# Attention 1: the maxima of the scores from 32 rows per head instead of 96

## The chip, the cores and the metric

The kernel runs on one core of a Trainium2 chip. The metric is the device time of one execution in microseconds, taken as the median of several runs. The whole kernel is one launch that computes eight sublayers one after the other (attention 1, a spiking feed-forward, a state space block and others); the change touches only the first, attention 1, which fills about the first 440 us of some 2070.

## The reference, cut to what matters

```python
# x: (2, 1024, 128); 16 heads of 64; latent of 32
q      = einsum('bld,dhk->blhk', x, Wq)
latent = einsum('bld,dc->blc',  x, Wkv_down)
k      = einsum('blc,chk->blhk', latent, Wk_up)
v      = einsum('blc,chk->blhk', latent, Wv_up)
attn   = einsum('bqhd,bkhd->bhqk', q, k) / 8
attn   = softmax(where(causal, attn, -big), axis=-1)
out    = einsum('bqhd,hdo->bqo', einsum('bhqk,bkhd->bqhd', attn, v), Wout)
```

The softmax needs a number per query that is near the maximum of its scores, so that no exponential overflows. Any number near the maximum gives the same result, since it is divided out again.

## The kernel before, in words

**Heads and halves.** Queries are multiplied by `Wk_up` beforehand, so that a head's query has only 32 numbers (`LD`) and all heads share the latent as keys. Four heads make a group `gg` (0 to 7: two batches of four groups). A group's queries come as one 128 x 512 product per half of the sequence (items "q"), rows 32h to 32h+31 for head h. ScalarE rounds it to the matmul's type (`qh`, high half) and VectorE takes what is left (`ql`, low half). Twelve DMAs per group (`s0_spread`, L474 to L476) lay these out as `qst`: for each head rows 0 to 31 high, 32 to 63 low, 64 to 95 high again, rows 96 and 97 the negated maximum in two halves. `kst` holds the latent in the same way (high, high, low, ones). One matmul over 96 rows thus gives the score with all three cross products, and over 128 rows the score less its maximum.

**Two kinds of work are woven into 96 steps.** A step `t` = (gg, c, n) handles half c of the queries (512) against block n of 128 keys, for the four heads. The numbers of steps below are t modulo 12: a group has steps 0 to 3 for c = 0 and 4 to 11 for c = 1. A step is: scores transposed, one matmul per head or two or four heads in one where the block is narrow (`scores`, L532, with a mask product L535 on the diagonal), exponentials on ScalarE (L695) from three PSUM banks in turn (3, 4, 5), and the products with the latent (`values`, L548, four heads in four groups of 32 columns), while GpSimd adds up the exponentials (L755).

Meanwhile the *items* prepare the maxima of the group that follows. "f" is a full block of 128 queries by 512 keys for one head: one matmul (L581) and one `tensor_reduce` on VectorE (L813). "d" is a block on the diagonal, r = 0 to 3 with width 128(r+1): four heads in one bank for r = 0, two for r = 1, one for r = 2 and 3; each is its product (L573), then a mask product (L576), then the reduce (L825). "n" transposes the negated maxima (L587), which then go to `qst` by DMA. "z" are the softmax sums (L599, L604), "y" the output. Items use PSUM banks 0, 1 and 2 in turn: item i waits until item i-3 has been read (`s0_af` at least i-2).

**The order is fixed by a plan.** `PLAN[t]` lists the items of a step, `plan(..., quota)` deals them out. In the turn of twelve steps that prepares a group they are, from step 3 on: 4, 4, 3, 3, 3, 3, 4, 4, 5, 5, 1, 1 items, to which come a "z" in steps 1 and 5 and a "q" in steps 10 and 11. The list is the 11 diagonal items of c = 0, "n", 16 full ones, 11 diagonal ones, "n". `parts(t)` cuts a step's items in thirds, and TensorE does: scores of two heads, first third, values of step t-1, second third, scores of the other two heads, last third. Before the steps there is an opening, which does the queries, latents and the maxima of group 0.

VectorE, ScalarE and GpSimd take the items in the same order, each on its own queue, with semaphores between them.

Of the kernel before, what the change touches and what calls it, by code (L numbers as in the profile page):

```python
# [7 lines left out]
ALU = mybir.AluOpType  # L8
# [6 lines left out]
P = 128  # L15
# [35 lines left out]
def f32(ap):  # L51
    return ap.bitcast(F32)


def build(nc, a, out, upto=8):

    ctx = ExitStack()
    with ctx:
# [281 lines left out]
        wkv4 = [tr(P), tr(P)]  # L340
        kst = tr(B, L)
        qst = [tr(2, 4, 512), tr(2, 4, 512)]
        qh = tr(2, 512)
        ql = tr(2, 512)
        nh = tr(2, P)
        nl = tr(2, P)

# [10 lines left out]
        s0_lat = sem("s0_lat")  # L358
        s0_khi = sem("s0_khi")
        s0_klo = sem("s0_klo")  # L360
        s0_latc = sem("s0_latc")
        s0_a = sem("s0_a")
        s0_qhi = sem("s0_qhi")
# [43 lines left out]

        def diagonal(gg, c):

            return [("d", gg, c, r, h, n) for r, n in ((0, 4), (1, 2), (2, 1), (3, 1)) for h in range(0, 4, n)]  # L410

        def full(gg):
            return [("f", gg, r, h) for r in range(4) for h in range(4)]
# [16 lines left out]
        for gg in range(2, NG0):  # L430
            t0 = 12 * (gg - 1)
            plan([("q", gg, 0), ("q", gg, 1)], (t0 - 2, t0 - 1), (1, 1))
            plan(diagonal(gg, 0) + [("n", gg, 0)] + full(gg) + diagonal(gg, 1) + [("n", gg, 1)],
                 range(t0 + 3, t0 + 15), (4, 4, 3, 3, 3, 3, 4, 4, 5, 5, 1, 1))
        for u, t in LAST.items():
            PLAN[min(t + 2, N_STEP + 1)].insert(0, ("z", u))
# [6 lines left out]
        def parts(t):  # L443

            x = PLAN[t]
            if len(x) == 1 and x[0][0] == "n":
                return [], [], x
            k = (len(x) + 2) // 3
            return x[:k], x[k:2 * k], x[2 * k:]

        def count_of(kind, i):
            return sum(1 for x in ITEMS[:i + 1] if x[0] == kind)
# [10 lines left out]
        def s0_spread(q):  # L463

            q.wait_ge(s0_pad, 4)
            for i, x in enumerate(ITEMS):
                if x[0] == "q" and x[2] == 1:
                    gg = x[1]
                    q.wait_ge(s0_af, i + 1)
                    if gg >= 2:  # L470
                        q.wait_ge(s0_e, SLOT_OF[12 * (gg - 1)])
                    for h in range(4):
                        rows = slice(LD * h, LD * h + LD)
                        q.dma_start(f32(qst[gg % 2][0:32, :, h, :]), f32(qh[rows])).then_inc(s0_qd, 16)  # L474
                        q.dma_start(f32(qst[gg % 2][32:64, :, h, :]), f32(ql[rows])).then_inc(s0_qd, 16)
                        q.dma_start(f32(qst[gg % 2][64:96, :, h, :]), f32(qh[rows])).then_inc(s0_qd, 16)  # L476
                if x[0] == "n":
                    _, gg, c = x
                    u = 2 * gg + c
                    q.wait_ge(s0_af, i + 1)  # L480
                    for row, part in ((96, nh), (97, nl)):
                        q.dma_start(f32(qst[gg % 2][row:row + 1, c, :, :].rearrange("o h (r q) -> o (h r) q", q=P)),
                                    f32(part[0:16, u % 2, :]).unsqueeze(1)).then_inc(s0_nd, 16)

        def s0_pe(pe):
# [53 lines left out]
            def values(t):  # L539
# [15 lines left out]
                                        start=n == 0, stop=n == 4 * c + 3, skip_group_check=True)  # L555
                ins.then_inc(s0_pv, 1)

            def item(x):
                i = AT[x]
                wait(pe, s0_af, i - 2)  # L560
                o = bank(i % 3)
                if x[0] == "q":
                    _, gg, k = x
                    b, g = gg // G0, gg % G0
                    ins = mm3(pe, o, (wq4[0][:, P * g:P * g + P], wq4[1][:, P * g:P * g + P]),
                              xt(L * b + 512 * k, 512))
                elif x[0] == "d":
                    _, gg, c, r, h, n = x
                    w = P * (r + 1)
                    pe.wait_ge(s0_qd, 192 * (gg + 1))  # L570
                    v = o[:, 0:n * w].rearrange("p (h k) -> p h k", h=n)
                    for k in range(n):
                        pe.matmul(v[:, k, :], qst[gg % 2][0:96, c, h + k, P * r:P * r + P],  # L573
                                  kst[0:96, gg // G0, 512 * c:512 * c + w], start=k == 0, stop=True,
                                  skip_group_check=True)
                    ins = pe.matmul(v[:, :, w - P:w], ident_bf[:, :],  # L576
                                    causal_bf[:, :].unsqueeze(1).to_broadcast([P, n, P]), start=False, stop=True,
                                    skip_group_check=True)
                elif x[0] == "f":
                    _, gg, r, h = x  # L580
                    ins = pe.matmul(o, qst[gg % 2][0:96, 1, h, P * r:P * r + P], kst[0:96, gg // G0, 0:512],  # L581
                                    start=True, stop=True)
                elif x[0] == "n":
                    _, gg, c = x
                    u = 2 * gg + c
                    pe.wait_ge(s0_m, u + 1)
                    ins = pe.matmul(o[0:16, 0:P], negf[:, u % 4, :], ident[:, :], start=True, stop=True)  # L587
                elif x[0] == "z":
                    u = x[1]
                    if (u // 2, u % 2) == PE_SUMS:  # L590
                        pe.wait_ge(s0_pv, N_STEP)
                        pe.sem_inc(s0_a, 1)
                        return
                    pe.wait_ge(s0_zp, ADDS_TO[LAST[u] + 1])
                    last = [t for t in range(LAST[u] - 2, LAST[u] + 1) if late(t)]
                    if last:
                        pe.wait_ge(s0_e, SLOT_OF[LAST[u] + 1])
                    for h in range(4):
                        ins = pe.matmul(o[LD * h:LD * h + LD, :], ones32, zacc[u % 2][:, h, :], start=True,  # L599
                                        stop=not last, skip_group_check=True)  # L600
                    for t in last:
                        c0, w = width(t)
                        for h in range(4):
                            ins = pe.matmul(o[LD * h:LD * h + LD, c0:512], ones32, pt[t % 4][:, h, 0:w], start=False,  # L604
                                            stop=t == LAST[u], skip_group_check=True)
                else:
                    _, b, k = x
                    pe.wait_ge(s0_ot, 2 * G0 * (b + 1) - (1 if k < 2 else 0))
                    for t in range(2):
                        for g in range(G0):  # L610
                            q0 = 256 * k + P * t
                            ins = pe.matmul(o[:, P * t:P * t + P], ot[:, g, q0:q0 + P], bcomb[:, g, :],
                                            start=t == 0 and g == 0, stop=g == G0 - 1, skip_group_check=True)
                ins.then_inc(s0_a, 1)
# [4 lines left out]
            latents(0)  # L619
            latents(1)  # L620
            pe.wait_ge(s0_klo, 2 * B)
            pe.wait_ge(s0_latc, B)
            pe.wait_ge(s0_pad, 4)
            for x in PLAN[-1][2:]:
                item(x)
            for t in range(N_STEP + 2):
                first, second, third = parts(t)
                own = range(len(slots(t))) if t < N_STEP else []
                for j in own[:2]:
                    scores(t, j)  # L630
                for x in first:
                    item(x)
                if 0 < t <= N_STEP:
                    values(t - 1)
                for x in second:
                    item(x)
                for j in own[2:]:
                    scores(t, j)
                for x in third:
                    item(x)  # L640

        def s0_act(act, link):
            act.preload_act_table_set("natural_log_exp_and_others")
# [25 lines left out]
            def latents(b):  # L669
                for i in range(2):  # L670
                    act.wait_ge(s0_lat, 3 * b + i + 1)
                    act.activation(kst[0:96, b, 512 * i:512 * i + 512], bank(LAT_BANK[b][i])[0:96],
                                   ACT.Copy).then_inc(s0_khi, 1)
                act.wait_ge(s0_lat, 3 * b + 3)
# [24 lines left out]
            def item(x):  # L699
                i = AT[x]  # L700
                if x[0] == "q":
                    _, gg, k = x
                    act.wait_ge(s0_a, i + 1)
                    wait(act, s0_qd, 192 * gg)
                    act.activation(qh[:, k, :], bank(i % 3), ACT.Copy).then_inc(s0_qhi, 1)
                if x[0] == "n":
                    _, gg, c = x
                    u = 2 * gg + c
# [53 lines left out]
        def s0_dve(dve, link):  # L762
# [13 lines left out]
            def item(x):  # L776
                i = AT[x]
                o = bank(i % 3)
                if x[0] == "q":
                    _, gg, k = x  # L780
                    dve.wait_ge(s0_qhi, count_of("q", i))
                    wait(dve, s0_qd, 192 * gg)
                    dve.tensor_tensor(ql[:, k, :], o, f32(qh[:, k, :]), ALU.subtract).then_inc(s0_af, 1)
                elif x[0] == "n":
                    _, gg, c = x
                    u = 2 * gg + c
# [27 lines left out]
                else:  # L814
# [2 lines left out]
                    dve.wait_ge(s0_a, i + 1)  # L817
                    v = o[:, 0:n * w].rearrange("p (h k) -> p h k", h=n)
                    if c == 0:
                        if r == 0 and u >= 4:  # L820
                            dve.wait_ge(s0_a, AT[("n", gg - 2, 0)] + 1)
                        at = negf[:, u % 4, :].rearrange("p (h r) -> p r h", r=4)[:, r, h:h + n]
                    else:
                        at = negp[:, gg % 2].rearrange("p (h r) k -> p r k h", r=4)[:, r, 1, h:h + n]
                    dve.tensor_reduce(at, v, AX, ALU.max, negate=True).then_inc(s0_af, 1)  # L825
                    if r == 3 and h == 3:
                        dve.wait_ge(s0_af, i + 1)
                        if c == 0:
                            dve.sem_inc(s0_m, 1)
# [2033 lines left out]
```

## Time and profile before

| | us |
|---|---|
| median of three runs | 2062.61 (2062.19 to 2077.53) |
| the profiled execution, its own time | 2070.39 |
| its span in the trace | 2068.6 |
| TensorE busy | 1821.4 (88%) |
| VectorE busy | 1598.4 (77%) |
| ScalarE busy | 1194.8 (58%) |
| GpSimd busy | 955.7 (46%) |

The steps of attention 1 run from about 62 us to 437 us. In the trace PE is the matmul stream, PEld the weight loads, DVE VectorE, ACT ScalarE, POOL GpSimd. A matmul's row tells its start and how long it was in flight; since matmuls are pipelined, what it costs the stream is the distance from its start to the start of the next one. `96*128` in a row means 96 rows by 128 columns of the array.

### The profile page before, as it was taken

The page shows a single profiled execution, that of the slowest core. Times are in us where ns is not written, and L with a number is a line of the kernel's source. Part 1 is how long each engine was busy: PE and PEld are TensorE (multiplying, and loading weights), DVE is VectorE, ACT ScalarE, POOL GpSimd, SP SyncE. Part 2 cuts the span into 40 slices and gives each one's busy share as a digit, 9 for nine tenths or more (in the row PEclk, how much of TensorE's full clock was granted, in tenths as well). Part 3 has the DMA queues.
Part 4 walks back from the last instruction along what each step waited for, and adds up shares of the span by engine and source line. Part 5 has one row for each costly group of instructions (what it writes and reads, how often), then busy time and mean ns, then how long its engine had stood idle before and what let it go on. Part 6 is the DMA issues. An engine that isn't in the chain of part 4 may idle for free.

```text
span 2068.6 us, 33172 instructions
## 1 busy us (share of the span) xinstructions
PE 1821.4 (88%) x12499; PEld 1206.3 (58%) x12499; DVE 1598.4 (77%) x2099; ACT 1194.8 (58%) x2056; POOL 955.7 (46%) x386
## 2 busy tenths in 40 slices
PE   6899999985889986999999888899887777999998
PEld 5444454454455675767777555556554545677776
DVE  4566656549689987677776899899999999777666
ACT  2354545533888821546555677776777666555554
POOL 3266556513297922010000388788989899300000
PEclk9799999997899996999999999999999999999999
DMA  3111211000122310011100000000001000101000
GB/s 87 32 32 32 52 34 41 1 12 1 64 90 84 103 36 16 20 32 31 31 16 1 1 2 2 1 1 2 1 2 32 1 2 2 46 16 31 16 16 21
DMA packets 39555, 53.98 MB, mean 26 GB/s; under 512 B 6179, under 2 KB 22790, under 8 KB 39398
## 3 DMA queue, kind: packets, MB, share of 16 engines
q1 hardware_dynamic: 38870, 50.82, 8.8%
q8 instruction: 101, 1.65, 0.4%
q10 hardware_dynamic: 528, 1.05, 0.2%
q14 instruction: 56, 0.46, 0.1%
HBM read 37.83 MB, written 1.18 MB: 19 GB/s over the span
## 4 chain that ended last, share of the span: by engine, by line
PE 54%; DVE 18%; issue 17%; POOL 4%; ACT 4%; DMA 1%; SPq 1%; DVEq 0%; ACTq 0%; POOLq 0%; PEldq 0%
PE ps L46 10%; PE ps L48 8%; PE ps L47 8%; DVE negm L2723 7%; PE ps L1696 3%; PE ps L532 3%; PE ps L548 3%; PE ps L581 2%; PE ps L573 2%; PE ps L2635 2%; PE ps L2552 2%; DVE AF L2730 2%; PE ps L1684 2%; POOL AR_plain L2528 1%; PE ps L2626 1%
## 5 line engine op out<-in xcount | busy, mean ns | idle before, releaser
L2723 DVE TENSOR_REDUCE negm<-ps 128x64 bf16<-128x1024 f32 x256 | 301.7, 1211 | 20.8 <-PE ps L2626 20.7
L2528 POOL TENSOR_TENSOR AR_plain<-AF 128x2048 f32<-128x2048 f32 x64 | 261.7, 4095 | 30.2 <-ACT AF L2679 30.2
L2687 ACT ACTIVATE AF<-ps 128x1024 f32<-128x1024 f32 x192 | 196.5, 1023 | 135.3 <-PE ps L2635 130.8
L46 PE MATMUL ps<-XH,AR 128*128 128x512 f32 x616 | 255.9, 415 | 16.6 <-DVE XL L251 5.9
L755 POOL TENSOR_TENSOR AF<-AF 128x2048 f32<-128x2048 f32 (+3 forms) x52 | 184.7, 3552 | 178.7 <-ACT AF L695 175.8
L47 PE MATMUL ps<-XL,AR 128*128 128x512 f32 x616 | 246.5, 400 | 0.0
L48 PE MATMUL ps<-XH,AR 128*128 128x512 f32 x616 | 246.5, 400 | 0.0
L695 ACT ACTIVATE AF<-ps 128x512 f32<-128x512 f32 (+1 forms) x304 | 154.1, 576 | 145.2 <-PE ps L532 69.7
L2635 PE MATMUL ps<-negm,ident_bf 128*128 128x512 bf16 x512 | 162.5, 401 | 78.3 <-DVE negm L2723 77.8
L2730 DVE TENSOR_REDUCE AF<-AF 128x128 f32<-128x2048 f32 x96 | 218.2, 2273 | 0.0
L285 POOL TENSOR_SCALAR var_eps<-mv 128x8 f32<-128x8 f32 x10 | 4.2, 421 | 376.2 <-DVE mv L262 376.1
L1955 DVE TENSOR_TENSOR_SCAN AF<-AF,ps 128x1024 f32<-128x1024 f32 x64 | 144.4, 2275 | 18.5 <-PE ps L1684 12.9
L1376 DVE TENSOR_TENSOR AF<-ps,AF 128x512 f32<-128x512 f32 x128 | 88.4, 691 | 89.7 <-ACT AF L1334 86.8
L1334 ACT ACTIVATE AR_plain<-ps 128x512 f32<-128x512 f32 x128 | 76.6, 598 | 135.3 <-PE ps L48 135.2
L1376 DVE TENSOR_TENSOR AR_plain<-ps,AR_plain 128x512 f32<-128x512 f32 x128 | 88.3, 690 | 85.2 <-ACT AR_plain L1334 85.1
L1334 ACT ACTIVATE AF<-ps 128x512 f32<-128x512 f32 x128 | 76.5, 598 | 132.6 <-PE ps L48 130.5
L2626 PE MATMUL ps<-AF_rounded,AR 128*128 128x256 f32 x704 | 149.7, 337 | 2.1 <-ACT AF L2687 2.0
L46 PEld LDWEIGHTS ps<-XH,AR 128*128 128x128 f32 x616 | 119.1, 193 | 54.1 <-issue 16.5
L2528 POOL TENSOR_TENSOR hc<-AF 128x2048 f32<-128x2048 f32 x32 | 131.1, 4098 | 12.1 <-ACT AF L2679 12.0
L48 PEld LDWEIGHTS ps<-XH,AR 128*128 128x128 f32 x616 | 119.1, 193 | 27.5
L47 PEld LDWEIGHTS ps<-XL,AR 128*128 128x128 f32 x616 | 119.6, 194 | 23.5
L2626 PEld LDWEIGHTS ps<-AF_rounded,AR 128*128 128x128 f32 x704 | 112.9, 199 | 33.2 <-ACT AF L2687 5.8
(329 smaller groups left out, 4245.1 us busy)
## 6 DMA issues: line engine op xcount, KB each, us to landing
AF<-scan_c_rows SPq DMA_DIRECT2D x32, 512.0 KB, 3.6
AR<-AR SPq DMA_DIRECT2D x96, 128.0 KB, 2.4
AF<-in_L_ffn_Wg_dram SPq DMA_DIRECT2D x21, 256.0 KB, 2.7
AF<-in_L_ffn_Wu_dram SPq DMA_DIRECT2D x21, 256.0 KB, 3.1
AF<-in_L_ffn_Wd_dram SPq DMA_DIRECT2D x21, 256.0 KB, 3.8
AF<-in_L_attn_a_Wq_dram SPq DMA_DIRECT2D x1, 512.0 KB, 4.2
AF<-in_L_attn_a_Wout_dram SPq DMA_DIRECT2D x1, 512.0 KB, 9.2
lnt<-in_L_ffn_W_fc_dram SPq DMA_DIRECT2D x2, 256.0 KB, 6.9
```

Source lines behind the costliest of these rows:

```text
L46: pe.matmul(out, ah, bh, start=start, stop=False)
L47: pe.matmul(out, ah, bl, start=False, stop=False)
L48: return pe.matmul(out, al, bh, start=False, stop=stop)
L695: act.activation(dst[:, h0:h0 + nh_, 0:w], bank(3 + e % 3)[:, 0:nh_ * w].rearrange("p (h q) -> p h q", h=nh_), ACT.Exp).then_inc(s0_e, 1)
L755: pool.tensor_tensor(zacc[u % 2][:, :, c0:512], zacc[u % 2][:, :, c0:512], pt[t % 4][:, :, 0:w], ALU.add).then_inc(s0_zp, 1)
L1376: dve.tensor_tensor(MH[k][m % 3], bank(2 + m % 2), MSG[k][m % 3], ALU.mult).then_inc(m_h, 1)
L2528: pool.tensor_tensor(p6[m % 3].rearrange("p (j q i) -> p j q i", j=HJ, i=2), e6[m % 4].rearrange("p (j q i) -> p j q i", j=HJ, i=2), w6i[: ...
L2626: ins = pe.matmul(bank(2 * (j % 3) + x // 2)[:, 256 * (x % 2):256 * (x % 2) + 256], k6[g // LB][:, x, P * kb:P * kb + P], q[:, :, q0:q0 + ...
L2635: ins = pe.matmul(bank(2 * (j % 3) + h).rearrange("p (j q i) -> p j q i", j=4, i=2), ident_bf[:, :], negm6[:, j % 4, :].unsqueeze(1).unsqu ...
L2687: act.activation(o[:, :, q0:q0 + 2 * SUB], bank(2 * (j % 3), 2).rearrange("p (j c) -> p j c", j=HJ), ACT.Exp).then_inc(s6_e, 1)
L2723: dve.tensor_reduce(negm6[:, j % 4, :], bank(2 * (j % 3), 2).rearrange("p (j q i) -> p q j i", j=HJ, i=2), mybir.AxisListType.XY, ALU.max, ...
L2730: dve.tensor_reduce(z6[:, m % 2, :], e6[m % 4].rearrange("p (j q i) -> p q j i", j=HJ, i=2), mybir.AxisListType.XY, ALU.add).then_inc(s6_z ...
```

## The change

The maxima of items "f", and of items "d" with one head (r = 2 and 3), are computed from the high halves alone: `qh`, rows 32h to 32h+31, against `kh4`, the latent's high half repeated for four heads on 128 rows. That is a product over 32 rows in place of 96. `qh` gets a second buffer. Two neighbouring "d" items are issued as product, product, mask, mask. The order of the diagonal items is turned round (r = 2, 3, 1, 0), "n" of c = 0 comes two full items later, and `parts` cuts steps of 2 to 6 items in twos (2, 2, rest), with a "z" counted extra.

```diff
-        qh = tr(2, 512)
+        qh = [tr(2, 512), tr(2, 512)]
+        kh4 = tr(B, L)
...
-            return [("d", gg, c, r, h, n) for r, n in ((0, 4), (1, 2), (2, 1), (3, 1)) for h in range(0, 4, n)]
+            return [("d", gg, c, r, h, n) for r, n in ((2, 1), (3, 1), (1, 2), (0, 4)) for h in range(0, 4, n)]
...
-            plan(diagonal(gg, 0) + [("n", gg, 0)] + full(gg) + diagonal(gg, 1) + [("n", gg, 1)],
+            plan(diagonal(gg, 0) + full(gg)[:2] + [("n", gg, 0)] + full(gg)[2:] + diagonal(gg, 1) + [("n", gg, 1)],
...
-            k = (len(x) + 2) // 3
-            return x[:k], x[k:2 * k], x[2 * k:]
+            z = 1 if x and x[0][0] == "z" else 0
+            k = 2 if 2 <= len(x) - z <= 6 else (len(x) - z + 2) // 3
+            return x[:z + k], x[z + k:z + 2 * k], x[z + 2 * k:]
...
+            def diagonal_products(x):
+                _, gg, c, r, h, n = x
+                w = P * (r + 1)
+                wait(pe, s0_af, AT[x] - 2)
+                if n == 1:
+                    rows = slice(LD * h, LD * h + LD)
+                    pe.wait_ge(s0_qhi, 2 * gg + c + 1)
+                    pe.matmul(heads(x)[:, 0, :], qh[gg % 2][rows, c, P * r:P * r + P],
+                              kh4[rows, gg // G0, 512 * c:512 * c + w], start=True, stop=True, skip_group_check=True)
+                else:
...
+            def part(xs):
...
+                    k = 2 if i + 1 < len(xs) and xs[i + 1][0] == "d" else 1
+                    for x in xs[i:i + k]:
+                        diagonal_products(x)
+                    for x in xs[i:i + k]:
+                        diagonal_mask(x)
...
                 elif x[0] == "f":
                     _, gg, r, h = x
-                    ins = pe.matmul(o, qst[gg % 2][0:96, 1, h, P * r:P * r + P], kst[0:96, gg // G0, 0:512],
+                    rows = slice(LD * h, LD * h + LD)
+                    pe.wait_ge(s0_qhi, 2 * gg + 2)
+                    ins = pe.matmul(o, qh[gg % 2][rows, 1, P * r:P * r + P], kh4[rows, gg // G0, 0:512],
                                     start=True, stop=True)
...
             pe.wait_ge(s0_klo, 2 * B)
+            pe.wait_ge(s0_k4, 2 * B)
...
                     act.wait_ge(s0_lat, 3 * b + i + 1)
+                    act.activation(kh4[:, b, 512 * i:512 * i + 512], bank(LAT_BANK[b][i]), ACT.Copy).then_inc(s0_k4, 1)
...
-                    wait(act, s0_qd, 192 * gg)
-                    act.activation(qh[:, k, :], bank(i % 3), ACT.Copy).then_inc(s0_qhi, 1)
+                    wait(act, s0_qd, 192 * (gg - 1))
+                    if gg >= 2:
+                        act.wait_ge(s0_a, AT[("n", gg - 2, 1)] + 1)
+                    act.activation(qh[gg % 2][:, k, :], bank(i % 3), ACT.Copy).then_inc(s0_qhi, 1)
...
-                    if r == 3 and h == 3:
+                    if r == 0:
                         dve.wait_ge(s0_af, i + 1)
```

## Rows read from the trace of the kernel before

**Rows 1.** Busy us by engine in one stretch, then clock, DMA share, GB/s.

```profile
...
150.00:200.00 50.00, 47.55 (x308) 23.60 (x306) 32.15 (x54) 26.32 (x54) 33.33 (x12) 1.00 0.16 33
...
```

**Rows 2.** The page: the granted clock of TensorE in 40 slices.

```profile
...
PEclk9799999997899996999999999999999999999999
...
```

**Rows 3.** Timeline of PE: an "n" of c = 0.

```profile
...
142.14 0.27 PE L587 MATMUL ps<-ident,AF 128*16 128x128 f32 x1 [0.62 <-DVEq L829]
...
```

**Rows 4.** Timeline, all engines: the same "n" one turn later.

```profile
...
185.45 0.19 PEld L532 LDWEIGHTS ps<-AR 128*128 128x128 f32 x1 [0.66 <-ACT AF L695]
...
186.58 0.27 PE L587 MATMUL ps<-ident,AF 128*16 128x128 f32 x1 [0.63 <-DVEq L829]
...
```

**Rows 5.** Timeline of PE, step of four items: start us, us in flight.

```profile
...
153.05 0.73 PE L581 MATMUL ps<-AR 96*128 96x512 f32 x2
153.62 0.34 PE L532 MATMUL ps<-AR 128*128 128x384 f32 x1
...
154.95 0.28 PE L535 MATMUL ps<-AF,ident_bf 128*128 128x256 bf16 x1
...
155.64 0.85 PE L548 MATMUL ps<-AF 128*32 128x384 f32 x8
...
```

**Rows 6.** Timeline of PE, later stage: a 64-row product between 128-row ones.

```profile
...
1089.25 0.39 PE L47 MATMUL ps<-XL,AR 128*128 128x512 f32 x1
1089.48 0.39 PE L48 MATMUL ps<-XH,AR 128*128 128x512 f32 x1
1089.80 0.50 PE L2328 MATMUL ps<-one,AR 64*128 64x512 f32 x1
1090.23 0.50 PE L46 MATMUL ps<-XH,AR 128*128 128x512 f32 x1
```

**Rows 7.** Timeline of a step of three items, all engines.

```profile
...
143.30 0.50 PE L581 MATMUL ps<-AR 96*128 96x512 f32 x1
...
143.65 0.63 PE L532 MATMUL ps<-AR 128*128 128x512 f32 x2
...
144.12 0.39 PE L581 MATMUL ps<-AR 96*128 96x512 f32 x1
...
144.73 0.19 PEld L532 LDWEIGHTS ps<-AR 128*128 128x128 f32 x1 [0.42 <-ACT AF L695]
...
145.06 0.40 PE L581 MATMUL ps<-AR 96*128 96x512 f32 x1
...
145.39 1.07 PE L548 MATMUL ps<-AF 128*32 128x512 f32 x8
...
```

**Rows 8.** Waits, 100 to 400 us: who <- whom: total us, times, longest.

```profile
...
PEld ps L581 <- DVE AF L813: 22.0, 28, 0.8
...
```

**Rows 9.** Timeline, opening: 64-row products on alternating halves of the rows.

```profile
...
24.63 1.68 PE L499 MATMUL ps<-AF 64*128 64x32 f32 x14
...
```

**Rows 10.** Timeline of PE, opening: 128-row products with a new load each.

```profile
...
41.64 0.38 PE L47 MATMUL ps<-AR,XH 128*128 128x32 f32 x1
41.85 0.37 PE L48 MATMUL ps<-AR,XL 128*128 128x32 f32 x1
```

**Rows 11.** Timeline of PE over two diagonal blocks with masks.

```profile
...
163.23 0.23 PE L576 MATMUL ps<-causal_bf,ident_bf 128*128 128x128 bf16 x1
163.39 0.42 PE L548 MATMUL ps<-AF 128*32 128x128 f32 x8
163.74 0.50 PE L573 MATMUL ps<-AR 96*128 96x512 f32 x1
...
164.49 0.48 PE L532 MATMUL ps<-AR 128*128 128x512 f32 x1
...
```

**Rows 12.** Groups, 0 to 480 us: count | busy us, mean ns.

```profile
...
L813 DVE TENSOR_REDUCE AF<-ps 128x1 f32<-128x512 f32 x128 | 84.2, 688 | 34.1 <-PE ps L581 32.8
...
L825 DVE TENSOR_REDUCE AF<-ps 128x1 f32<-128x384 f32 x64 | 32.8, 550 | 2.7 <-PE ps L576 2.3
...
```

**Rows 13.** Timeline of ScalarE at the end of the opening.

```profile
...
44.60 0.38 ACT L675 ACTIVATE AF<-ps 128x256 f32<-128x256 f32 x1 [2.20 <-PE ps L48]
```

More of the change, by code:

```diff
@@ L360, in build @@
         s0_klo = sem("s0_klo")
+        s0_k4 = sem("s0_k4")
         s0_latc = sem("s0_latc")
@@ L473, in s0_spread @@
                         rows = slice(LD * h, LD * h + LD)
-                        q.dma_start(f32(qst[gg % 2][0:32, :, h, :]), f32(qh[rows])).then_inc(s0_qd, 16)
+                        q.dma_start(f32(qst[gg % 2][0:32, :, h, :]), f32(qh[gg % 2][rows])).then_inc(s0_qd, 16)
                         q.dma_start(f32(qst[gg % 2][32:64, :, h, :]), f32(ql[rows])).then_inc(s0_qd, 16)
-                        q.dma_start(f32(qst[gg % 2][64:96, :, h, :]), f32(qh[rows])).then_inc(s0_qd, 16)
+                        q.dma_start(f32(qst[gg % 2][64:96, :, h, :]), f32(qh[gg % 2][rows])).then_inc(s0_qd, 16)
                 if x[0] == "n":
@@ L556, in values, with heads, diagonal_mask @@
                 ins.then_inc(s0_pv, 1)
+            def heads(x):
+                _, gg, c, r, h, n = x
+                w = P * (r + 1)
+                return bank(AT[x] % 3)[:, 0:n * w].rearrange("p (h k) -> p h k", h=n)
+            def diagonal_products(x):
+                _, gg, c, r, h, n = x
+                w = P * (r + 1)
+                wait(pe, s0_af, AT[x] - 2)
[5 more added lines that the diff above has]
+                else:
+                    pe.wait_ge(s0_qd, 192 * (gg + 1))
+                    for k in range(n):
+                        pe.matmul(heads(x)[:, k, :], qst[gg % 2][0:96, c, h + k, P * r:P * r + P],
+                                  kst[0:96, gg // G0, 512 * c:512 * c + w], start=k == 0, stop=True,
+                                  skip_group_check=True)
+            def diagonal_mask(x):
+                _, gg, c, r, h, n = x
+                w = P * (r + 1)
+                pe.matmul(heads(x)[:, :, w - P:w], ident_bf[:, :],
+                          causal_bf[:, :].unsqueeze(1).to_broadcast([P, n, P]), start=False, stop=True,
+                          skip_group_check=True).then_inc(s0_a, 1)
+            def part(xs):
+                i = 0
+                while i < len(xs):
+                    if xs[i][0] != "d":
+                        item(xs[i])
+                        i += 1
+                        continue
+                    k = 2 if i + 1 < len(xs) and xs[i + 1][0] == "d" else 1
[3 more added lines that the diff above has]
+                        diagonal_mask(x)
+                    i += k
             def item(x):
@@ L566, in item @@
                               xt(L * b + 512 * k, 512))
[L567 to L578, printed above, removed]
                 elif x[0] == "f":
                     _, gg, r, h = x
-                    ins = pe.matmul(o, qst[gg % 2][0:96, 1, h, P * r:P * r + P], kst[0:96, gg // G0, 0:512],
+                    rows = slice(LD * h, LD * h + LD)
+                    pe.wait_ge(s0_qhi, 2 * gg + 2)
+                    ins = pe.matmul(o, qh[gg % 2][rows, 1, P * r:P * r + P], kh4[rows, gg // G0, 0:512],
                                     start=True, stop=True)
@@ L621, in s0_pe @@
             pe.wait_ge(s0_klo, 2 * B)
+            pe.wait_ge(s0_k4, 2 * B)
             pe.wait_ge(s0_latc, B)
             pe.wait_ge(s0_pad, 4)
-            for x in PLAN[-1][2:]:
-                item(x)
+            part(PLAN[-1][2:])
             for t in range(N_STEP + 2):
@@ L630, in s0_pe @@
                     scores(t, j)
-                for x in first:
-                    item(x)
+                part(first)
                 if 0 < t <= N_STEP:
                     values(t - 1)
-                for x in second:
-                    item(x)
+                part(second)
                 for j in own[2:]:
                     scores(t, j)
-                for x in third:
-                    item(x)
+                part(third)
         def s0_act(act, link):
@@ L782, in item @@
                     wait(dve, s0_qd, 192 * gg)
-                    dve.tensor_tensor(ql[:, k, :], o, f32(qh[:, k, :]), ALU.subtract).then_inc(s0_af, 1)
+                    dve.tensor_tensor(ql[:, k, :], o, f32(qh[gg % 2][:, k, :]), ALU.subtract).then_inc(s0_af, 1)
                 elif x[0] == "n":
@@ L819, in item @@
                     if c == 0:
-                        if r == 0 and u >= 4:
+                        if r == 2 and h == 0 and u >= 4:
                             dve.wait_ge(s0_a, AT[("n", gg - 2, 0)] + 1)
```

## The prediction

> **What bounds the kernel now.** The change is in attention 1, so I read that stage and not the whole page. First the sums by stretch: between 150 and 200 us TensorE is busy 47.55 of 50 us, VectorE 32.15, ScalarE 26.32, GpSimd 33.33, at a full granted clock [rows 1]; from the third slice to the eighth the clock is full, or nearly [rows 2]. The stage is set by TensorE's stream, and VectorE has a third to spare. Then one turn of twelve steps: the same "n" starts at 142.14 and at 186.58 us, so a turn takes 44.4 us, and some seven turns hold the items that the change touches [rows 3, 4]. Then the timeline of single steps, for what one item costs the stream. In a step of four, two full items and the way to the next score take 153.05 to 153.62, 0.57 us, and two more, from the mask ahead of them to the values, 154.95 to 155.64, 0.69 us [rows 5]. Fully streamed, 512 columns cost 0.23 us (1089.25 to 1089.48) [rows 6]; where the load of the weights is not hidden, 0.11 us more (143.30 to 143.65, 0.35 us, is the same product straight after the values) [rows 7]. The waits list adds that loads of full items waited 28 times for VectorE's reduces, 22.0 us of PEld's time; most of this lies beside running matmuls [rows 8].
>
> **What a product over 32 rows costs.** The number of rows does not shorten the stream, the columns do. Two things change. *Gain:* two heads sit on different rows and can run together. In the opening, 64-row products alternate between the halves of the array: 14 of them took 1.68 us, each 0.40 in flight, so (1.68 - 0.40)/6 = 0.21 us for two [rows 9]; 128-row products with a new load each take 0.21 us for one (41.64 to 41.85) [rows 10]. In flight they are equally long (0.40 and 0.37), which speaks for one clock in both. So I take a pair of heads at the price of one. *Loss:* the array is cut differently than for the 128-row products around it. Where a 64-row product follows a 128-row one in a later stage, it starts 0.32 us after it and not 0.23, and its successor 0.43 us later [rows 6]: the load is not done ahead, and about 0.1 us goes by on top, on the way in and on the way out. From score over pair to values thus costs 0.32 + 0.11 + 0.43 = 0.86 us from one stream start to the next, where two 96-row heads with hidden loads cost 3 x 0.23 = 0.70. No row shows 32 rows of this type beside one another; the bounds are the pair at full overlap and the pair at two prices.
>
> The Trainium skill speaks for the change here: "TensorE: Matmul & The Clock Gate", Part 3, has tiles on other row groups start about 4 ns apart and counts nothing for going in and out of the tiling. By that page alone every pair would save its second head, which is the second rival below; the trace has the overlap [rows 9] but also the price at the borders [rows 6].
>
> **The sum, per turn** (items by step as the plan deals them; steps modulo 12):
> - Steps 9 and 10, four full items each, in two pairs. After the values the array is recut anyway: 0.43 + 0.11 = 0.54 for the 0.57 of before. Ahead of the values: the way out of a 256-wide mask 0.21 (0.16 behind a 128-wide one, 163.23 to 163.39 [rows 11], and 0.05 for the columns), and 0.43, is 0.64 for 0.69. Together 4 pairs: -0.16.
> - Steps 7 and 8, three items, now cut 2, 1, 0 and not 1, 1, 1. The single item after the values costs 0.54 to the next score's stream for 0.35: +0.19. The pair ahead of the values makes 0.86 of the 0.66 from 144.73 to 145.39: +0.20. The item between the scores goes, 0.23, but 0.15 of that was no cost: the last score's load stands until 144.73 for an exponential, where 144.12 + 2 x 0.23 = 144.58 would do [rows 7]. So +0.31 each, +0.62.
> - Step 6: "n" stood ahead of the values and waited for VectorE: 185.45 to 186.58, 1.13 us, where a score takes 0.33 [rows 4]: 0.80 us of stall. Two items later it waits for nothing. Against it a pair ahead of the values, 0.86 - 0.33 = 0.53, and the third item gone, -0.08, as above; "n" itself costs what the full item in its place did. -0.35.
> - Diagonal pairs, seven in a turn. Before, two 512-wide heads with masks take 163.74 to 164.49, 0.75 us [rows 11]. After: load 0.11, stream 0.21, border 0.1, two masks 0.1 = 0.52, and 0.1 for the way in behind a mask, in about half of them. On the mean of 512 and 384 wide -0.15 each, -1.0.
> - New waits on VectorE. The second head of a pair needs the bank that the first head of the pair before has left, and a reduce takes 0.69 us [rows 12], about 0.2 after the product. In step 4 only values of 128 columns lie between, 163.39 to 163.74, 0.35 us [rows 11]: 0.2 + 0.69 + 0.05 - 0.16 - 0.35 = 0.4. Steps 3 and 11 have shorter reduces of 384 columns, 0.55 us [rows 12], and wider values between, and come to 0.1 each; behind the waiting head stand its masks, and the scores of the step. +0.6.
> - Two diagonal heads that find no partner (r = 3 of c = 1): 0.1 in, 0.1 out and a load of 0.11 uncovered, +0.6 together.
> - The narrow diagonal items behind "z": the same items at another place. VectorE takes "z" first as before; I put +0.2 for the reduce of r = 1 that step 5's second part waits for, between 0 and 0.7 (a whole reduce).
>
> That is +0.5 us a turn, times seven, +3.5. **The opening:** ScalarE's four further copies of 0.6 us lie in its idle 2.20 us before the last latent copy and in the one before [rows 13]; nothing, and up to +1.2 if the latents came earlier. Its diagonal items are bound by VectorE at half clock; "product, product, mask, mask" hands over the first of two later, 0.2 to 0.4 us for eight pairs there and in the first steps: +2.5. The twelve DMAs of a group stay; products from `qh` no longer wait for them, but that wait is covered before. Sum **+6 us**. The profiled execution took 2070.39 us and would take 2076; it stands 8 above the median of 2062.61, which would be **2069 us**.
>
> **The rivals.**
> - *The borders cost nothing extra* for 32 rows of this type, or the loads go ahead after all. Then steps 7 and 8 come to about 0, the others gain 0.2 to 0.3 a pair, and the waits on exponentials and reduces keep half of it: about -1.5 a turn, 2052 us. Against it: all 64-row products in the later stage show the border.
> - *The second head is free and nothing waits:* 14 pairs x 0.3 us (0.23 to 0.38 of before) x 7 = -29 us, 2033. For it: VectorE has 18 of 50 us left [rows 1]. Against it: the waits of steps 4, 7 and 8 above, and ScalarE's in 144.73.
> - *Slower: the heads do not overlap.* The second head has its own semaphore wait and its own bank; if its load starts only when the first has streamed, each pair costs 0.21 us more than summed. 14 x 0.21 x 7 = 21 us, to 2090. It decides against the kernel from about half of the pairs onward. This is also the case in which the change does not do what its name says. Against it: the 64-row pairs of the opening [rows 9].
> - *Slower: the clock.* TensorE streams less per step. In the opening, where full items are spaced by VectorE's reduces, the clock was at its half level (the second slice, 0.7) [rows 2]. Should a tenth of the steps fall to 1.2 GHz, with steps of some 5 us in place of 3.5, that is 10 steps x 1.5 = +15 on top, 2084 or more.
>
> **Chances.** The forecast (a few us slower, borders paid, pairs overlapping) 0.5; borders free 0.21; all free 0.08; no overlap 0.12; clock 0.06; the rest lies beside these. A measurement of this kernel tells about 1% (20 us) from no change. Faster by more than that needs the second rival: 0.09. Slower by more needs no overlap or the clock: 0.13. Within 1%: 0.78. The range of 8 in 10 goes from 2048, below the first rival, to 2086, most of the way to the third.
>
> **What would show it.** Right: starts of two L581-type products within some 10 ns, of different heads; 0.32 from a score to a pair and 0.43 from the pair to the next load; the stall before "n" of c = 0 gone; a turn of 44.5 to 45.5 us; reduces idle for the first of each pair, and the second head of step 4's second pair late by 0.4. Wrong: pairs 0.1 or 0.2 us apart (no overlap), loads of the scores begun while a pair streams (borders free), a turn under 43 us, or half-clock stretches between 90 and 400 us.

## The result, and the profile after

The changed kernel took **2091.54 us** (median; 2084.20 to 2094.83) where the kernel before, run again beside it, took 2065.22. The two medians lie 26 us apart; the ratio of all executions is 1.011, with a 95% interval of 1.0086 to 1.0134. I had forecast 2069 and a range from 2048 to 2086. A loss of more than 1% I had given 0.13.

The page after, against [rows 2]: the span (before 2068.6), the busy times and the granted clock.

```profile
span 2089.1 us, 33302 instructions
...
PE 1836.6 (88%) x12499; PEld 1197.6 (57%) x12499; DVE 1594.2 (76%) x2099; ACT 1197.7 (57%) x2060; POOL 955.4 (46%) x386
...
PEclk9599999998799998899999999999999999999999
```

TensorE is busy 15 us more, and VectorE 4 us less. In the clock line the second slice has fallen from 7 to 5. To see where the 20.5 us of span went I cut both traces at the start of the values of each step 0. First the changed kernel, then the one before. The columns are start and end, length, PE busy (x instructions), granted clock, DMA share, GB/s.

```profile
71.40:133.90 62.50, 57.66 (x302) 0.80 0.07 16
133.90:180.90 47.00, 44.35 (x277) 0.96 0.15 33
180.90:226.20 45.30, 43.08 (x281) 1.00 0.18 39
226.20:272.60 46.40, 44.39 (x279) 0.96 0.18 38
272.60:327.90 55.30, 52.87 (x345) 0.94 0.14 30
327.90:373.10 45.20, 43.00 (x281) 1.00 0.17 36
373.10:417.70 44.60, 42.69 (x275) 0.96 0.07 16
```

```profile
70.20:124.10 53.90, 49.12 (x299) 0.91 0.06 13
124.10:168.50 44.40, 42.00 (x288) 1.00 0.19 40
...
257.30:308.40 51.10, 49.16 (x349) 1.00 0.15 32
308.40:352.80 44.40, 41.99 (x288) 1.00 0.17 37
352.80:396.40 43.60, 40.28 (x278) 1.00 0.10 21
```

Two things are added. A turn at full clock is 45.2 to 45.3 and not 44.4 us, about 0.85 us more in each of seven, 6.0 us. And the clock: the kernel before had it full (2.4 GHz) from the second turn on. The changed one has stretches at the half level (1.2 GHz) in four of the six later turns, 17.1 us in all. Those six turns take 11.5 us more than before, 6.4 us beyond the 0.85 each. The opening takes 1.2 us more and the first turn 8.6, of which 7.75 beyond the 0.85; both also run longer at half clock (51.2 us between 45 and 115 us for 34.1). 1.2 + 7.75 + 6.0 + 6.4 is the 21.3 us at the last cut.

The single prices came out nearly as summed. The rows show a pair of full items between a score and the values, then a single one behind the values, then a pair behind the values (TensorE alone, three windows; the x2 rows of L616 are two products of different heads, whose starts are 3 to 4 ns apart):

```profile
152.32 0.51 PE L535 MATMUL ps<-AR 128*128 128x512 f32 x1 [0.22 <-ACT AF L728]
152.76 0.50 PE L616 MATMUL ps<-AR 32*128 32x512 f32 x2
153.19 0.64 PE L551 MATMUL ps<-AF 128*32 128x512 f32 x4
...
157.41 0.50 PE L616 MATMUL ps<-AR 32*128 32x512 f32 x1
157.84 0.73 PE L535 MATMUL ps<-AR 128*128 128x512 f32 x2
...
164.51 0.50 PE L616 MATMUL ps<-AR 32*128 32x512 f32 x2
164.94 0.44 PE L535 MATMUL ps<-AR 128*128 128x384 f32 x1
```

Two heads in flight for 0.50 us together are one head's time. The pair gives way to the next load after 0.43 us (152.76 to 153.19), and a single one takes the same 0.43 (157.41 to 157.84). That is 0.54 to the stream of the next product, since the load of 0.11 stands open: the two scores behind it are in flight for 0.73 us, where the same two in [rows 7] took 0.63. Before it was 0.35 [rows 7]. From score to values the pair takes 0.87 us (152.32 to 153.19), for the 0.86 of the sum. So the prices read from [rows 6] and [rows 9] held.

The waits of the changed kernel's turn (four rows of all engines, then two of TensorE alone):

```profile
187.40 0.28 PE L585 MATMUL ps<-causal_bf,ident_bf 128*128 128x128 bf16 x2
187.67 1.02 DVE L860 TENSOR_REDUCE AF<-ps 128x1 f32<-128x384 f32 x2 [0.22 <-PE ps L585]
188.36 0.30 PEld L535 LDWEIGHTS ps<-AR 128*128 128x128 f32 x2 [0.85 <-DMA AR<-AR]
188.36 0.50 PE L535 MATMUL ps<-AR 128*128 128x512 f32 x1 [0.68 <-DMA AR<-AR]
...
190.03 0.94 PE L573 MATMUL ps<-AR 32*128 32x512 f32 x2
190.90 0.28 PE L585 MATMUL ps<-causal_bf,ident_bf 128*128 128x128 bf16 x2
```

The first score of step 4 now stands still for the DMA of the negated maxima, 0.68 us. The same two places in the kernel before, "n" and score:

```profile
173.29 0.38 PE L587 MATMUL ps<-ident,AF 128*16 128x128 f32 x2 [0.58 <-DVE AF L833]
...
176.92 0.71 PE L532 MATMUL ps<-AR 128*128 128x512 f32 x2
```

From "n" to the score it is 3.55 us after (184.81 to 188.36) and 3.63 before. Before, TensorE's own work filled that time and the score had no wait. After, the work in between is shorter and the wait is open. At 190.03 the second head of the pair waits for the reduce (0.94 us for two, starts 0.44 apart): the wait that the sum put at 0.4 us in step 4.

### The profile page after: what moved, and what is told of

It is laid out like the page before. It is cut to its first block, busy times and chain, and to the rows that moved or that the text cites. A ratio compares the mean times of both kernels' runs of the same rounds, so it can differ in the third digit from the quotient of the medians.

```text
span 2089.1 us, 33302 instructions
## 1 busy us (share of the span) xinstructions
PE 1836.6 (88%) x12499; PEld 1197.6 (57%) x12499; DVE 1594.2 (76%) x2099; ACT 1197.7 (57%) x2060; POOL 955.4 (46%) x386
## 4 chain that ended last, share of the span: by engine, by line
PE 53%; DVE 18%; issue 18%; POOL 5%; ACT 4%; DMA 1%; SPq 0%; DVEq 0%; ACTq 0%; POOLq 0%; PEldq 0%
PE ps L46 10%; PE ps L48 8%; PE ps L47 8%; DVE negm L2758 7%; PE ps L535 4%; PE ps L1731 3%; PE ps L551 2%; DVE AF L2765 2%; PE ps L1719 2%; PE ps L573 2%; PE ps L616 2%; POOL AR_plain L2563 1%; PE ps L2670 1%; PE ps L2587 1%; PE ps L973 1%
## 5 line engine op out<-in xcount | busy, mean ns | idle before, releaser
L535 PE MATMUL ps<-AR 128*128 128x512 f32 (+1 forms) x304 | 124.6, 480 | 13.7 <-DMA AR<-AR 8.5
```

What stands on the lines that cost most here:

```text
L535: ins = pe.matmul(o, kst[:, gg // G0, P * n:P * n + P], qst[gg % 2][:, c, h0:h0 + nh_, c0:512], start=True, stop=True)
```

## The experiments

All comparisons are with the kernel before on the same chip in the same hours. "Half clock" is the time at 1.2 GHz between 115 and 400 us of the one profiled execution; a turn is the distance of two "n" or two values at full clock, leaving out the first, the fifth (it also has the output items) and the last.

| kernel | median us | ratio (95%) | turn | half clock |
|---|---|---|---|---|
| before | 2065 to 2073 | 1 | 44.4 | 0 |
| changed | 2091.5 | 1.011 (1.0086 to 1.0134) | 45.2 | 17.1 |
| 96 rows, new order | 2074.5 | 1.0024 (1.0010 to 1.0038) | 44.8 | 6.8 |
| 32 rows, old order, no pairs | 2131.6 | 1.0298 (1.0256 to 1.0340) | 47.9 | 61.9 |
| 32 rows, old order, diagonal pairs | 2103.0 | 1.0162 (1.0116 to 1.0208) | 47.2 | 0.3 |
| group 0 computed twice | 2098.8 | 1.0138 (1.0119 to 1.0158) | 45.3 | 13.7 |
| group 0 over 96 rows | 2085.9 | 1.0094 (1.0064 to 1.0124) | 45.2 | 17.1 |
| all heads on rows 0 to 31 | 2107.9 | 1.0182 (1.0156 to 1.0208) | 47.1 | 19.2 |
| 64 rows, same rows | 2101.9 | 1.0150 (1.0121 to 1.0180) | 47.1 | 6.8 |
| wait filled | 2083.4 | 1.0067 (1.0039 to 1.0095) | 45.3 | 0 |
| group 0 over 96 rows, wait filled | 2074.3 | 1.0017 (0.9999 to 1.0035) | 45.3 | 6.8 |
| before, "n" two items later | 2067.9 | 0.9994 (0.9977 to 1.0012) | 43.8 | 0.3 |
| early pair | 2066.2 | 0.9976 (0.9958 to 0.9993) | 43.3 | 6.8 |
| early pair, wait filled | 2065.4 | 0.9961 (0.9948 to 0.9975) | 43.3 | 0 |

Where the half-clock stretches fall differs from one execution to the next. For all executions of a kernel only the mean granted clock is there. As the clock has two levels here, twice what it lacks to 1, times the span, is an estimate of the half-clock time in the whole program: 198 to 207 us for the kernel before, 233 for the changed one (mean 0.944), 204 over 96 rows, 226 with group 0 over 96 rows, 216 with the wait filled, 197 with both, 294 for the old order without pairs.

**The order alone.** Products over 96 rows in the changed kernel:

```diff
-                    pe.matmul(heads(x)[:, 0, :], qh[gg % 2][rows, c, P * r:P * r + P],
-                              kh4[rows, gg // G0, 512 * c:512 * c + w], ...)
+                    pe.matmul(heads(x)[:, 0, :], qst[gg % 2][0:96, c, h, P * r:P * r + P],
+                              kst[0:96, gg // G0, 512 * c:512 * c + w], ...)
...
```

> The changed kernel with its order, its cutting of the steps and its product-product-mask-mask, but every product over 96 rows from the old layout, so no recutting of the array and no overlap of heads. Theory A (the 32-row products are the cost: borders in each turn, and a slower clock): about the time of before or a few us under it, 2055 to 2068, turns of about 44 us, the first turn 54 like before, no half-clock spells between 100 and 400 us. Rival B (order and cutting are the cost): it stays at 2085 to 2095, turns of 45 us and more.

Measured 2074.5, turns of 44.8 us, and one stretch at half clock, in the second turn. So order and cutting cost 0.4 us a turn, 0.24% in all; the 32-row products the other 0.9%. Theory A holds for most of it, not for all: I had expected the order to be worth a gain.

This run also has the wait for the DMA, and a longer one. The score of step 4 in its third turn:

```profile
181.84 0.50 PE L535 MATMUL ps<-AR 128*128 128x512 f32 x1 [0.81 <-DMA AR<-AR]
```

So the new order is enough to make the standstill; it does not need the 32-row products. In this execution TensorE stood still for 0.77 to 1.02 us there in five turns, and no half clock followed; the one stretch began at the wait of 1.55 us in the second turn. In the changed kernel, waits of 0.66 to 0.69 us were followed by half clock in three turns of five, and one of 1.32 us in the second turn too. The standstill alone does not bring half clock, then; with the 32-row products around it, it did.

**The 32 rows alone.** Old order, old thirds, `k = 1` in `part`.

> The kernel before with nothing but the 32-row products (and their copies of the latent): old order of items, old cutting in thirds, each product with its mask at once. Theory A: each item now pays two borders alone, where pairs are not adjacent; 16 full items and 16 diagonal ones a turn, the full ones in steps of three cost 0.2 to 0.38 us each: 3 us or so a turn, and the clock spells: 2095 to 2115. Rival B: the products are harmless, 2060 to 2070.

Measured 2131.6, above the range expected, and the largest loss of all. Turns at full clock are 47.9 us, 3.5 more than before, as expected, but the clock is at its half level for 62 us between 115 and 400 us (granted clock 0.89) and almost all the way from 45 to 115.

```profile
45.00:115.00 70.00, 64.79 (x196) 0.52 0.11 24
115.00:400.00 285.00, 278.08 (x1534) 0.89 0.14 29
```

Not every stretch here has a standstill ahead of it: the ones that begin at 218 and 371 us have no idle time of TensorE over 0.22 us in the 6 us before them.

**Old order with diagonal pairs** (`k = 2` in `part` where two diagonal items are neighbours):

> The kernel before with the 32-row products and with product-product-mask-mask for neighbouring diagonal items, but the old order and the old cutting in thirds, in which full items of steps of three stand alone. Theory A: between the changed kernel (2091) and the one without pairs of diagonal items (2132): the diagonal pairs save about 0.15 us each where two stand in one third, 4 of them a turn, so 2115 to 2128, with half-clock time before 450 us of 100 us and more. Rival B (order alone decides): 2125 to 2135.

Measured 2103.0 (two executions), its profiled execution shorter still (span 2093.8), with turns of 47.2 us. The range expected was 2115 to 2128. The pairs save 0.7 us a turn, 4 x 0.17. The other 24 us to the kernel without them fit the clock, which stayed full from 115 to 400 us in this trace; over all executions the estimate is 240 us at half clock for 294. Why four pairs a turn are worth so much of the clock is not shown.

**TensorE kept busier in the opening:**

```diff
+                    if gg == 0:
+                        pe.wait_ge(s0_qd, 192)
+                        for _ in range(1):
+                            pe.matmul(o, qst[0][0:96, 1, h, P * r:P * r + P], kst[0:96, 0, 0:512],
+                                      start=True, stop=True)
```

> The changed kernel, in which each full item of group 0 (opening and the first two steps) is computed twice: first over 96 rows, then over 32 into the same bank; the first is thrown away. TensorE waits for VectorE there, so that the added 0.21 us (0.43 at half clock) should be hidden. Theory C (TensorE does too little in the opening, so the clock stays at half for 37.5 us instead of 23.9 and again for 13.7): more work brings the full clock earlier, half-clock time before 110 us falls from 51 us towards 34, and the kernel gains 3 to 8 us: 2084 to 2089. Rival D (the time of the opening is set by waits and the clock follows it): no gain or 2 to 4 us of loss.

A loss, 2098.8. Half-clock time between 45 and 115 us fell only from 51.2 to 47.8 us, and the values of step 0 began at 83.0 instead of 71.4 us: the full items of the opening came 0.85 us apart, where the changed kernel has 0.60, so at half clock the added product did not fit between two reduces. The first turn then took 58.2 us for 62.5. More work in the opening is not the cure when it is in the way.

**The opening over 96 rows:**

```diff
+                    if gg == 0:
+                        pe.matmul(heads(x)[:, 0, :], qst[gg % 2][0:96, c, h, P * r:P * r + P], ...)
+                    else:
                         pe.matmul(heads(x)[:, 0, :], qh[gg % 2][rows, c, P * r:P * r + P], ...)
```

> The changed kernel, but the items of group 0 (opening and first three steps) over 96 rows; the other groups over 32 rows. Theory A: the first turn comes back from 62.5 us to about 54 to 56, 2082 to 2086, and what is left over before (15 to 20 us) is the turns and their clock. Rival: the first turn stays at 60 or more, since order and pairing set it, 2090.

First turn 57.8 us, start of the values 69.4: 6.7 us back of the 8.6 + 1.2, with 37.5 us at half clock between 45 and 115 us for 51.2. The later turns kept their stretches at half clock, 17.1 us. The opening's share is thus 32-row products and half clock together; which leads I did not take apart.

**What the overlap is worth:** `qh[gg % 2][0:LD, ...]` and `kh4[0:LD, ...]` for all four heads.

> The changed kernel with all heads' maxima taken from rows 0 to 31 (head 0's query for all four, so that this part of the computation is not the reference's): same shapes, order and borders, but the two heads of a pair cannot run together. It prices the overlap. Theory A: pairs start 0.2 us apart and not 0.004, 14 pairs of 0.21 us in 7 turns and some in the opening: plus 15 to 22 us, turns of 47 to 48 us; less where a wait on VectorE or ScalarE lay behind the pair. Rival E (behind each pair something else is waited for): under +8 us.

TensorE, a pair ahead of the values, here with both products on the same rows:

```profile
166.22 0.73 PE L616 MATMUL ps<-AR 32*128 32x512 f32 x2
166.88 0.64 PE L551 MATMUL ps<-AF 128*32 128x512 f32 x4
```

0.66 us to the values, for 0.43 with the overlap. A turn is 47.1 us, 1.9 more than the changed kernel's, and the median 16 us more, as expected. The overlap is real, and of the 14 x 0.21 = 2.9 us that it takes from the stream, two thirds reach the turn.

**Rows or time?** The same over rows 0 to 63 of `qst` and `kst` for every head:

> The changed kernel with the maxima of full and wide diagonal items over 64 rows (high and low halves of the queries against the latent's high half, the same 64 rows for every head): borders as over 32 rows, no overlap, twice the rows at work. Against the kernel with all heads on rows 0 to 31 (2108, turns of 47.10 us at full clock). Theory A (the price is the border and the missing overlap, not the number of rows): the same turn, 47.1 us. Rival F (the clock counts rows at work): fewer half-clock spells than its 82 us before 450 us, 5 to 15 us faster.

The turn is the same, 47.1 us, so 32 rows cost this turn what 64 do. The stretches at half clock are 6.8 us for 19.2. But that is one trace of each, and such stretches vary from execution to execution; by the mean granted clock it is 239 us for 247 in the whole program, over two and four executions. That the clock counts the rows at work is neither shown nor refuted.

**The wait filled:**

```diff
-                if n == 0:
-                    pe.wait_ge(s0_nd, 32 * (2 * gg + c + 1))
                 wait(pe, s0_e, e - 2)
                 o = bank(3 + e % 3)[:, 0:nh_ * w].rearrange("p (h q) -> p h q", h=nh_)
+                if n == 0:
+                    if c == 1 and j == 0:
+                        for _ in range(4):
+                            pe.matmul(o, kst[0:96, gg // G0, 0:P], qst[gg % 2][0:96, c, h0:h0 + nh_, c0:512],
+                                      start=True, stop=True)
+                    pe.wait_ge(s0_nd, 32 * (2 * gg + c + 1))
```

> The changed kernel with four products of 96 rows by 512 columns, thrown away, in front of the first score of each half c = 1, where TensorE waits 0.9 us for the DMA of the negated maxima. They fill a wait and add nothing the kernel needs. Theory C (half-clock spells start where TensorE's stream stands still in this stretch; each costs 1.2 to 3 us): the spells between 100 and 400 us are gone, all turns but the fifth take 45.2 to 45.4 us, and the kernel gains 4 to 6 us: 2085 to 2088. Rival D (spells come from the 32-row products as such): spells stay, 2091 to 2096.

The four added products stand where TensorE stood still (timeline of TensorE, then the two stretches of this kernel, and those of the changed one):

```profile
185.66 0.28 PE L589 MATMUL ps<-causal_bf,ident_bf 128*128 128x128 bf16 x2
185.75 1.18 PE L536 MATMUL ps<-AR 96*128 96x512 f32 x4
186.76 0.63 PE L539 MATMUL ps<-AR 128*128 128x512 f32 x2
```

```profile
45.00:115.00 70.00, 63.62 (x238) 0.63 0.11 24
115.00:400.00 285.00, 275.49 (x1778) 1.00 0.16 35
```

```profile
45.00:115.00 70.00, 63.01 (x234) 0.63 0.11 24
115.00:400.00 285.00, 271.41 (x1715) 0.97 0.16 35
```

The second to fourth and the sixth turn are now 45.3 us each, with the clock full from 115 to 400 us; opening and first turn are as they were. The six later turns take 6.5 us less than in the changed kernel, which is the 6.4 put down to the clock. The median is 8 us lower with *more* work on the busiest engine (the intervals of the two ratios, 1.0039 to 1.0095 and 1.0086 to 1.0134, just overlap), and over all executions the estimate of half-clock time falls from 233 to 216 us, by the same 17 us as in the trace. In the changed kernel's trace each of the four stretches began 0.9 to 2.9 us after this standstill ended; with it filled there were none.

**Both cures:**

> The changed kernel with both cures at once: group 0 over 96 rows and the thrown-away products in the DMA wait. If the two parts of the loss are separate (opening about 6 us, spells about 8), it comes to 2076 to 2080, half-clock time before 450 us as in the kernel before (34 to 55 us), every turn from the second on 45.2 to 45.4 us; what is left over the kernel before is then 7 turns of 0.9 us, 6 to 8 us. If they are one effect (the clock anywhere), it is not better than the filled one, 2083.

2074.3, ratio 1.0017 (0.9999 to 1.0035). The changed kernel's 1.1% falls to about 0.2%. The two parts are separate: the cures alone took 6 and 8 us off the median, both together 17, somewhat more than their sum. What is left is 3.5 us where seven turns of 0.85 would be 6. One stretch at half clock remained in this trace behind 115 us, from 120.2 to 127.0, in the first turn; TensorE had no idle time over 0.22 us in the 18 us before it, so the standstill is not the only way to one.

**Before, with "n" of c = 0 two items later:**

```diff
-            plan(diagonal(gg, 0) + [("n", gg, 0)] + full(gg) + diagonal(gg, 1) + [("n", gg, 1)],
+            plan(diagonal(gg, 0) + full(gg)[:2] + [("n", gg, 0)] + full(gg)[2:] + diagonal(gg, 1) + [("n", gg, 1)],
```

> The kernel before, only with the transpose of the maxima of c = 0 two full items later (from group 2 on). In the changed kernel this edit took the 0.8 us stall ahead of it away. Theory: a turn of 44.4 falls by 0.3 to 0.7 us in the six turns that have it, -2 to -4 us, 2060 on the chip where the kernel before takes 2063: ratio 0.998 to 0.999. Rival: the wait for VectorE only moves to the next item, since VectorE is 0.8 us behind there, ratio 1.000.

The trace has the gain, turns of 43.8 for 44.4 us, 0.6 each. The times alone do not show it: 0.9994, 0.9977 to 1.0012. If this 0.6 also holds in the changed kernel, the rest of its order and cutting costs about 1.0 us a turn, an estimate from this and the 0.4 of the run over 96 rows.

**A version that beats both.** From these: 96 rows, old thirds, "n" later, and only one 32-row pair a turn, where TensorE waits anyway. The diagonal items are turned round for c = 0 alone.

```diff
+            order = ((2, 1), (3, 1), (1, 2), (0, 4)) if c == 0 else ((0, 4), (1, 2), (2, 1), (3, 1))
...
+            PLAN[t0 + 2][:0] = diagonal(gg, 0)[:2]
...
+            plan(diagonal(gg, 0)[2:] + full(gg)[:2] + [("n", gg, 0)] + full(gg)[2:] + diagonal(gg, 1) + [("n", gg, 1)],
+                 range(t0 + 3, t0 + 15), (4, 4, 3, 3, 3, 3, 4, 4, 4, 4, 1, 1))
```

> A version meant to beat both: the kernel before with 96 rows, its cutting in thirds, the transpose of c = 0 two full items later, and only two 32-row products per turn, side by side, done in step 2, where TensorE waits for the transpose of c = 1 (1.44 us of values for 0.78), so that steps 11 and 0 have four items for five. Theory: the pair hides in the wait, and the two lighter steps save 0.3 us each on top of the 0.6 of the transpose: turns of 43.1 to 43.4 us, 2056 to 2062, ratio 0.995 to 0.998. Rival: the reduces of the pair delay the chain transpose, DMA, score, and steps with the reversed order of c = 0 lose what is won: turns of 44 and more, ratio 1.000 or above.

2066.2 against 2070.3, ratio 0.9976 (0.9958 to 0.9993), its turns 43.3 to 44.1 us but for the first, the one with the output items, the last (41.6), and one of 46.9 with a stretch at half clock. With two filling products before the DMA wait:

> The version with the early pair, with two products of 96 rows, thrown away, ahead of the first score of each half c = 1, where TensorE waits for the DMA. In its trace one spell of 6.8 us at half clock cost the sixth turn 3 us. Theory C (the spells start in this standstill): no spell between 100 and 400 us, all full turns 43.3 to 43.6 us, 1 to 3 us less in the median than without: ratio 0.995 to 0.998. Rival: the spells of this version are rare, the added products cost some 0.1 us a turn where the wait is short, ratio 0.998 to 1.000.

2065.4 against 2072.5, **0.9961 (0.9948 to 0.9975)**, the turns 43.3 to 44.0 us but for the first, the one with the output items and the last, and the clock full from 115 to 400 us. Both versions are faster than the kernel before by a small and clear amount. That the filling products help here is not shown: the intervals of the two ratios overlap.

```profile
45.00:115.00 70.00, 63.84 (x302) 0.81 0.11 24
115.00:400.00 285.00, 276.39 (x1845) 1.00 0.16 35
```

## Why the prediction was wrong

- **Borders and overlap**: right. 0.43 us from a pair or a single one to the next load, starts 4 ns apart; the kernel without overlap puts the overlap at 1.9 us a turn. The rival without overlap is refuted, and so are the two with free borders. One premise was weaker than it read: "one clock in both" went by the times in flight, while the profile gives a granted clock of 1.00 for 24 to 27 us and 0.50 for 40 to 42 us. The page "TensorE: Matmul & The Clock Gate", Part 3, of the Trainium skill is right on the overlap (4 ns) and silent on what the change of tiling takes.
- **The sum per turn**: +0.5 forecast, +0.85 measured at full clock, 7 turns, 6 us for 3.5. Two of its terms can be seen: values of step 3 to values of step 4 grew from 4.12 to 4.82 us (wait on VectorE, and the r = 1 items ahead of the values), and with the stall before "n" gone the next distance of values went from 4.36 to 3.95. Missing was a cost of the order: over 96 rows it already costs 0.4 a turn, though the "n" move alone gains 0.6.
- **The DMA wait was missed.** I costed the cheaper diagonal items in steps 2 and 3 as a gain. From the values with "z" to the score of step 4 it is 10.6 us before and after (166.29 to 176.92, then 177.80 to 188.36): before, TensorE's stream just filled the chain "z", "n", DMA, score, and after it the chain alone sets that time. What was saved there became 0.68 us of standstill in front of the score. The new order is enough for that, as the run over 96 rows shows (0.81).
- **The step that failed: the clock.** The sum held the clock constant, and a rival with 0.06 had it fall. It fell: 6.4 of the 11.5 us lost in the six later turns, which the filled wait gave back, and part of the loss in opening and first turn. There the half-clock time grew by 17 us, and in the first turn alone from 10 to 25 us; at the later turns' price (6.4 us for 17.1) those 15 us are worth some 5.6 us, an estimate. So the rival's 15 us on top was about right for the clock's whole share (12 us by this estimate); its chance was not. What brings the half level is open. It took the 32-row products: over 96 rows, the same order with longer waits has no more half-clock time than the kernel before (204 us by the mean clock, for 202). In the later turns the standstill is part of it, since filling it removed the stretches; elsewhere stretches began without one.
- **The opening**: +2.5 forecast, about +9 measured with the first turn (1.2 + 7.75), of which group 0 over 96 rows gave 6.7 back. The term left out the longer half-clock time. That the products of a pair and their masks go out later is argued, and its share not measured.

## What to carry to other kernels

On TensorE a saved matmul is worth nothing where a chain over other engines or a DMA sets the time, and it can cost: here the standstill it left was followed by half clock in four turns of six, and thrown-away products in that place gave some 8 us back. Small row tiles pay side by side, but each step into a tiling, and each out of it again, cost some 0.2 us here, which made 0.86 of 0.70 for a pair; count borders, not only products. Before a change that shortens the stream of the busiest engine, list which waits come next and what the granted clock did after each of them.

## What the runs showed of the hardware that was not expected

- Added work on the busiest engine can make a kernel faster: four thrown-away products of 0.25 us in a standstill of 0.7 us, once per group, took all 17 us at half clock away between 115 and 400 us of the trace.
- Two 32-row products on different rows, 4 ns apart, are in flight 0.50 us together; on the same rows 0.73. Single products over 32 and over 64 rows cost the same, turns of 47.1 us.
- TensorE can fall to the half level without a standstill over 0.22 us ahead of it (218 us in the old order without pairs, 120 us with both cures), and it can stand still for 0.77 to 1.02 us in five turns without falling (the new order over 96 rows).
- With group 0 over 96 rows, the trace has 37.5 us at half clock between 45 and 115 us without the filled wait and 30.7 with it. Up to 72.5 us both have 23.9; the difference lies in the first turn, where one of them has the filling products.
